# Token marks as three wide VectorE operations per set, in a decoder layer on one Trainium2 core

## The reference

```
logits = flat @ router_w.T + router_b
topk_vals, topk_idx = jax.lax.top_k(logits, TOP_K)       # 2 of 8 experts for each token
topk_w = jax.nn.softmax(topk_vals, axis=-1)
for e in range(n_exp):
    cw = jnp.sum(jnp.where(topk_idx == e, topk_w, 0.0), axis=-1)
    y = jax.nn.gelu(flat @ w1[e].T + b1[e], approximate=False)
    y = y @ w2[e].T + b2[e]
    out = out + y * cw[:, None]
x = _layernorm(x + _layernorm(out + hidden_states, ln_w, ln_b))
```

## Time and profile before

| | |
|---|---|
| median of 3 runs | 536.84 us (535.76 to 541.52) |
| the profiled execution | 537.01 us, its span 535.2 us |
| busy in the span | PE 496.5 us, PEld 446.6, DVE 367.2, ACT 261.7, POOL 268.9 |
| mean granted TensorE clock | 0.981 |

### The profile page before, as it was taken

One profiled execution on the slowest core, in us unless ns is written; L12 is line 12 of the kernel. 1 busy time (PEld: TensorE's weight loads), 2 busy tenths in 40 slices (PEclk: granted clock), 3 DMA queues, 4 the chain that ended last, 5 costly groups with the idle time before them and its releaser, 6 DMA issues.

```text
span 535.2 us, 10956 instructions
## 1 busy us (share of the span) xinstructions
PE 496.5 (93%) x3286; PEld 446.6 (83%) x3286; DVE 367.2 (69%) x1088; ACT 261.7 (49%) x861; POOL 268.9 (50%) x409
## 2 busy tenths in 40 slices
PE   5888999989999899998699999999999999999981
PEld 4667888878888788998598999999999999999970
DVE  4778867857676876448976656766676666676674
ACT  3455577765767567653233444343444334444420
POOL 4553232232332432246357657775667666676564
PEclk9899999999999999999989999999999999999997
DMA  8019930645465826445265566665566666666320
GB/s 231 12 30 352 292 107 12 234 140 168 167 198 175 276 54 252 145 167 177 90 208 198 178 208 213 223 210 204 190 199 218 226 211 225 210 202 219 138 51 1
...
## 3 DMA queue, kind: packets, MB, share of 16 engines
...
q10 hardware_dynamic: 1632, 0.27, 0.3%
...
## 4 chain that ended last, share of the span: by engine, by line
PE 34%; POOL 19%; DVE 18%; issue 17%; DMA 5%; ACT 3%; POOLq 1%; ACTq 0%; SPq 0%; DVEq 0%
PE psum_b L1569 6%; PE psum_v L1702 5%; PE psum_a L1668 5%; POOL out L809 4%; POOL routing L805 4%; POOL work L801 3%; POOL work L796 3%; POOL front_then_w_ring L752 3%; DMA weighed_outputs<-work 2%; PE psum_m L1720 2%; DVE routing L1435 2%; PE psum_b L1818 2%; PE psum_m L1569 2%; DVE work L1451 1%; PE psum_c L1689 1%
## 5 line engine op out<-in xcount | busy, mean ns | idle before, releaser
L1024 ACT ACTIVATE front_then_w_ring<-psum_b,front_then_w_ring 128x128 f32<-128x128 f32 x160 | 45.6, 368 | 72.6 <-PE psum_b L1818 72.6
L1024 ACT ACTIVATE front_then_w_ring<-psum_a,front_then_w_ring 128x128 f32<-128x128 f32 x152 | 43.2, 368 | 72.6 <-PE psum_a L1818 72.6
L1818 PEld LDWEIGHTS psum_b<-front_then_w_ring 128*128 128x128 f32 x640 | 74.5, 192 | 0.9
L1818 PE MATMUL psum_b<-front_then_w_ring 128*128 128x128 f32 x640 | 75.1, 275 | 0.0
L1818 PEld LDWEIGHTS psum_a<-front_then_w_ring 128*128 128x128 f32 x608 | 73.2, 198 | 0.9
L1818 PE MATMUL psum_a<-front_then_w_ring 128*128 128x128 f32 x608 | 73.6, 281 | 0.0
L1841 PE MATMUL psum_v<-expert_w,front_then_w_ring 128*128 x320 | 72.6, 380 | 0.2 <-issue 0.2
L912 ACT ACTIVATE work<-psum_a,score_max 128x77 f32<-128x77 f32 x256 | 62.2, 335 | 17.6 <-DVE score_max L1193 17.4
L1841 PE MATMUL psum_c<-expert_w,front_then_w_ring 128*128 x304 | 68.9, 380 | 0.1
L1841 PEld LDWEIGHTS psum_v<-expert_w,front_then_w_ring 128*128 128x128 f32 x320 | 59.5, 191 | 7.5 <-issue 0.4
L1841 PEld LDWEIGHTS psum_c<-expert_w,front_then_w_ring 128*128 128x128 f32 x304 | 56.4, 190 | 7.2 <-issue 0.4
...
## 6 DMA issues: line engine op xcount, KB each, us to landing
...
```

What stands on the lines that cost most here:

```text
L1024: last = act.activation(hidT[t % 2][:, c, :], src[:, n, q * P:(q + 1) * P], ACT.Gelu, bias=bias[:, c:c + 1])
L1818: last = pe.matmul(dst[:, n, q * P:(q + 1) * P], w1[:, k, c * P:(c + 1) * P], xtT[t % 2][:, k, :], start=(k == 0), stop=(k == KD - 1))
```

## The change

All pairs of a set are marked by three `tensor_tensor` operations over 128 x 128 x pairs elements in place of two `tensor_scalar` operations per pair: `mark_positions` and `mark_columns` compare a table of column numbers with the parts, `mark_tokens` multiplies by the token numbers in place. All operands have 2 bytes: `cols`, `token1` and `part_n` become float16, and `cols` repeats each number nine times, which makes one POOL iota of 1152 elements out of one of 128. The pair is now the innermost index of both mark arrays, so that a pair's matrix has a step of 14 or 18 elements (28 or 36 bytes) from column to column where PE reads it.

The order changes too. On PE `ranks(LAST)` moves behind `turn_rows(3)` and `down(1)`, set 1's `mark_pairs` moves behind `up(5)`, and `turn_last_tokens` behind `up(38)`. On DVE `sum_row(0)` moves ahead of `rest_map`, `sum_row(1)` ahead of `indices(3)`, and the marks of set 1 stand in two places, one operation behind `indices(3)` and two behind `sum_row(2)`. ACT, POOL and SP keep their order.

```diff
@@ -64,7 +64,7 @@
 RANKS_AT = 384
 LOGITS_AT = 320
 SET_PAIRS = tuple(TOPK * n for _, n in SETS)
-MARK_GROUPS = tuple(tuple((c * n + a, c * n + b) for c in range(TOPK) for a, b in ((0, (n + 1) // 2), ((n + 1) // 2, n))) for _, n in SETS)
+MARK_STEPS = 3
 EPS = 1e-5
 EPS_FFN = 1e-12
 MASKED = -1e30
@@ -300,8 +300,8 @@
 
         rev = tmp(E)
         slot_base = tmp(E)
-        cols = tmp(P, dt=F16)
-        token1 = tmp(TILES)
+        cols = tmp(P, TILES - FIRST, dt=F16)
+        token1 = tmp(TILES, dt=F16)
         token_off = tmp(TILES)
         tau = tmp(XS_TILES, E - 1)
         tau_row = tau[:, :, 0]
@@ -325,12 +325,12 @@
         higher = tmp(TILES, E)
         slot_i = tmp(TOPK, TILES, dt=I32)
         part_i = tmp(TOPK * TOPK, TILES, dt=I32)
-        part_n = tmp(TOPK * TOPK, TILES)
+        part_n = tmp(TOPK * TOPK, TILES, dt=F16)
         ext = tmp(TILES, E, EXT)
         mark_words = SET_PAIRS[0] * P // 2
 
         def marks(ap):
-            return ap.bitcast(F16).rearrange("p (i m) -> p i m", m=P)
+            return ap.bitcast(F16).rearrange("p (m i) -> p m i", m=P)
 
         late_words = SET_PAIRS[1] * P // 2
         at_pos = [marks(LATE[:, 0:mark_words]), marks(SECOND[:, 0:late_words])]
@@ -672,7 +672,7 @@
                       allow_small_or_imprecise_dtypes=True).then_inc(route_consts, 1)
             pool.iota(slot_base, pattern=[[PER_E * P, E]], base=1, channel_multiplier=0,
                       allow_small_or_imprecise_dtypes=True).then_inc(route_consts, 1)
-            pool.iota(cols, pattern=[[1, P]], base=0, channel_multiplier=0,
+            pool.iota(cols, pattern=[[1, P], [0, TILES - FIRST]], base=0, channel_multiplier=0,
                       allow_small_or_imprecise_dtypes=True).then_inc(route_consts, 1)
             pool.iota(token1, pattern=[[P, TILES]], base=1, channel_multiplier=1,
                       allow_small_or_imprecise_dtypes=True).then_inc(route_consts, 1)
@@ -1241,8 +1241,12 @@
                 if H == RANKS_STEP + 8:
                     dve.wait_ge(pos_mm, 1)
                     dve.tensor_copy(first_token_of, table_psum(0)).then_inc(table_ready, 1)
-                if RANKS_STEP + 3 <= H < RANKS_STEP + 3 + len(MARK_GROUPS[0]):
-                    mark_rows(0, *MARK_GROUPS[0][H - RANKS_STEP - 3])
+                if H == RANKS_STEP + 3:
+                    mark_positions(0)
+                if H == RANKS_STEP + 4:
+                    mark_columns(0)
+                if H == RANKS_STEP + 5:
+                    mark_tokens(0)
             steps = [0]
 
             def then(ins):
@@ -1370,17 +1374,34 @@
                 dve.wait_ge(map_ready, MAPS)
                 map_of(tbend, spare, XS_TILES, e_base)
 
-            def mark_rows(n, first_pair, end):
+            def pairs_of(ap, n):
+                return ap.rearrange("p m (c t) -> p m c t", c=TOPK)
+
+            def over_pairs(n):
+                return [P, P, TOPK, SETS[n][1]]
+
+            def numbers(n):
+                nt = SETS[n][1]
+                return cols[:, :, 0:nt].rearrange("p m (c t) -> p m c t", c=1).to_broadcast(over_pairs(n))
+
+            def parts(n, half):
                 t0, nt = SETS[n]
+                part = part_n[:, half * TOPK:(half + 1) * TOPK, t0:t0 + nt]
+                return part.rearrange("p (m c) t -> p m c t", m=1).to_broadcast(over_pairs(n))
+
+            def mark_positions(n):
                 if n == 0:
                     dve.wait_ge(qT_ready, NP)
-                for i in range(first_pair, end):
-                    c, j = divmod(i, nt)
-                    t = t0 + j
-                    dve.tensor_scalar(at_pos[n][:, i], cols, part_n[:, c, t:t + 1], None, ALU.is_equal)
-                    last = dve.tensor_scalar(at_col[n][:, i], cols, part_n[:, TOPK + c, t:t + 1], token1[:, t:t + 1],
-                                             ALU.is_equal, ALU.mult)
-                last.then_inc(pos_ready, 1)
+                dve.tensor_tensor(pairs_of(at_pos[n], n), numbers(n), parts(n, 0), ALU.is_equal).then_inc(pos_ready, 1)
+
+            def mark_columns(n):
+                dve.tensor_tensor(pairs_of(at_col[n], n), numbers(n), parts(n, 1), ALU.is_equal).then_inc(pos_ready, 1)
+
+            def mark_tokens(n):
+                t0, nt = SETS[n]
+                tokens = token1[:, t0:t0 + nt].rearrange("p (m c t) -> p m c t", m=1, c=1).to_broadcast(over_pairs(n))
+                dve.wait_ge(pos_ready, n * MARK_STEPS + 2)
+                dve.tensor_tensor(pairs_of(at_col[n], n), pairs_of(at_col[n], n), tokens, ALU.mult).then_inc(pos_ready, 1)
 
             for p in range(3):
                 input_moments(p)
@@ -1474,19 +1495,17 @@
             first_hot(LAST)
             second_choice(LAST)
             dve.memset(token_of[:, P:COLS], 0.0)
+            sum_row(0)
             rest_map()
             ranked(LAST)
             place(LAST)
             dve.wait_ge(ln_in, 2 * 16)
             weigh_output(1)
             add_input(1)
-            sum_row(0)
-            mark_rows(LAST, *MARK_GROUPS[LAST][0])
             row(inner_norm(0))
+            sum_row(1)
             indices(3)
-            sum_row(1)
-            mark_rows(LAST, *MARK_GROUPS[LAST][1])
-            mark_rows(LAST, *MARK_GROUPS[LAST][2])
+            mark_positions(LAST)
             def last_tokens():
                 dve.wait_ge(load_ready, SLOT_TILES)
                 for n in range(2):
@@ -1529,7 +1548,8 @@
                 add_input(t)
                 sum_row(t)
                 if t == 2:
-                    mark_rows(LAST, *MARK_GROUPS[LAST][3])
+                    mark_columns(LAST)
+                    mark_tokens(LAST)
                     later_map()
                 if t == FIRST - 4:
                     dve.wait_ge(pos_mm, LAST + 1)
@@ -1773,10 +1793,9 @@
                 last.then_inc(rank_mm, 1)
 
             def mark_pairs(n):
-                for g, (first_pair, end) in enumerate(MARK_GROUPS[n]):
-                    pe.wait_ge(pos_ready, n * len(MARK_GROUPS[0]) + g + 1)
-                    for i in range(first_pair, end):
-                        last = pe.matmul(table_psum(n), at_pos[n][:, i], at_col[n][:, i], start=(i == 0), stop=(i == SET_PAIRS[n] - 1))
+                pe.wait_ge(pos_ready, (n + 1) * MARK_STEPS)
+                for i in range(SET_PAIRS[n]):
+                    last = pe.matmul(table_psum(n), at_pos[n][:, :, i], at_col[n][:, :, i], start=(i == 0), stop=(i == SET_PAIRS[n] - 1))
                 last.then_inc(pos_mm, 1)
 
             normalised(0)
@@ -1862,23 +1881,21 @@
             up(2, 0)
             route_logits(TILES - 1)
             up(2, 1)
-            pe.wait_ge(lg_ready, TILES)
-            ranks(LAST)
             turn_rows(3)
             down(1)
+            ranks(LAST)
             for t in range(3, SLOT_TILES):
-                if t == FIRST - 2:
-                    pe.wait_ge(placed, 3 * LAST + 1)
-                    mark_pairs(LAST)
                 up(t, 0)
                 up(t, 1)
+                if t == FIRST - 2:
+                    mark_pairs(LAST)
+                if t == LAST_TILE:
+                    turn_last_tokens()
                 if t + 1 < SLOT_TILES:
                     turn_rows(t + 1)
                 if t - 1 == FIRST:
                     pe.wait_ge(map_ready, 2 * MAPS)
                 down(t - 1)
-                if t == LAST_TILE - 1:
-                    turn_last_tokens()
             down(SLOT_TILES - 1)
```

## The result

| | before | after |
|---|---|---|
| median of 4 runs | 537.10 us (535.76 to 541.52) | 548.96 us (548.12 to 550.00) |
| profiled execution | 537.01 us, span 535.2 | 548.74 us, span 547.0 |
| PE / DVE / POOL busy | 496.5 / 367.2 / 268.9 | 505.0 / 360.3 / 277.5 |
| mean granted clock | 0.981 | 0.970 |

The ratio is 1.0207 (95%: 1.0169 to 1.0244): slower by 11.9 us, where no change was forecast. The marks did get cheaper, and VectorE is busy 7 us less. The time went elsewhere.

The account below looks back on a forecast made before the run. The chain from `weigh_output(3)` through tile 7's gather was taken to bound the stretch, TensorE from there on. 537.01 + 0.0 (A) - 1.1 (B) + 2.4 (C) - 1.2 (D) = 537.1; forecast 537.0 us, range 531.5 to 541.5.

Parts of the forecast that it names:

- The iota, costed at nothing: Among GpSimd's early constants: the longer iota is free since GpSimd idles half the span; 1.1 us without that cover.
- A, the strided product: Set 0, attention loop: wide marks gain 0.3 us, strided product costs 0.3; 0.0 in all (-0.5 to +3.6).
- signs of being wrong: Tile 7's gather issued before 274 us, marks over 2 us, or mark products over 0.1 us apart.
- B, tile 7: Set 1: fewer marks between `sum_row(1)` and `weigh_output(3)` bring `turn_rows(7)` earlier; gain of 1.1 us, capped by a gather.
- C, the clock: TensorE waits 5.8 us ahead of `turn_rows(7)` and its clock falls uncovered behind it: +2.4 us (0 to 3.6).
- D, the end: Kernel end: `up(38)` covers the 1.76 us wait of `turn_last_tokens`, last weighing earlier: -1.2 us (-2 to 0).
- The slower one: Wide marks at one element a step also hold GpSimd's gathers: 542.3 us, 544.7 with a clock fall; chance 0.08.

Follow-up runs that it names:

- e2: The changed kernel with its iota of 1152 elements moved into an idle GpSimd stretch of the attention loop; 543.12 us, ratio 1.0092.
- e7: e2 with set 1's rank product and the sums of rows 0 and 1 back in their old places; 541.80 us, ratio 1.0073.
- e9: The kernel before with wide marks and strided product in set 1 only, later mark product and last-token transpose, longer iota at 102 us; 534.56 us, ratio 0.9953.
- e1: The kernel before with its iota writing 1152 elements as nine runs of 128; 538.45 us, ratio 1.0042.
- e5: The kernel before plus the change's own iota (each number nine times in a row) into a tile nothing reads; 544.76 us, ratio 1.0107.
- g2: e7 with set 0's strided mark product issued twice; 545.65 us, ratio 1.0124.
- e6: The kernel before with its narrow marks stored with the change's step between elements; 547.97 us, ratio 1.0179.
- g1: e9 with set 0's dense mark product issued four times; 537.27 us, ratio 0.9977.
- e4: The kernel before with narrow marks in their old layout, but all the change's moves on PE and DVE; 542.98 us, ratio 1.0101.
- d1: The kernel before with only `turn_last_tokens` moved behind `up(38)`; 537.12 us, ratio 0.9965.
- e3: The changed kernel with marks stored pair by pair, a zero step in the wide operations, iota back to 128 elements; 543.65 us, ratio 1.0119.

## Why the prediction was wrong

The moves in the medians of all runs, one edit after the other: 549.0 after, 543.1 with the iota moved (e2), 541.8 with ranks and row sums back (e7), 534.6 with set 0 as before (e9). Two terms of the sum carry the miss, the iota and the strided product of set 0.

**The iota, costed at nothing: +6.0 us.** This is the first step that failed. The prediction put the longer iota under "GpSimd is idle for half of the span", and priced it without that cover at 1.1 us. Both were wrong, and for different reasons. The cover is a mean over the span; at 37 us POOL goes from the constants to the key weighing without a pause, and PE waits for it. I never looked at the row. And the price of 1.04 ns an element was VectorE's. It is near GpSimd's only for long runs: 9 runs of 128 took 1.13 us (e1), where 128 elements took 0.23, but 128 runs of 9 took 3.75 (e5). The iotas behind the dear one overlap it in the trace, and from L660 to the key weighing it is 3.5 us more in all. The rest is the clock, which falls behind the longer wait. e5 and e2 show it from both sides.

**A, the strided product: +0.8 us in the profile and about 7 in the medians, where 0.0 was forecast.** The marks were right: 1.22 us against 1.1, and c-d grows by 2.0 us, so without the product's 2.5 it gains 0.5 (0.3 forecast). Part of the 2.5 is hidden, since PE would have waited for the first gather of token rows. The product was taken at 0.3, near the lower end of 0 to 2.4, and the upper end was true. The argument for the lower end, that float32 products keep to 0.12 us, says nothing about a step: those read without one. By the Trainium skill, "SBUF — State Buffer", section "Specifications (TRN2)", an access that gets less than two hits out of a 16-byte line is slowed; with steps of 28 and 36 bytes there is one. The trace agrees: 0.23 us against 0.056. The prediction cited that rule and did not let it move the term, though products over 0.1 us apart stand among its own signs of being wrong.
What the section on A did not have at all: the clock can fall behind such a product (e2, g2), 3 us more. With it A is 4 us; the other 3 of the 7 us between e7 and e9 are not accounted for.

**B, tile 7: +1.8 us where -1.1 was forecast.** By its own steps: from `sum_row(1)` to `weigh_output(3)` 15.1 us were forecast, 15.8 came (marks of 1.55 us, not 1.35). But `sum_row(1)` was to be 0.25 us later and was 2.6 (15.26 against 12.68 behind the choice). The sentence that failed is that VectorE's wait "is filled by `sum_row(0)`". It took the gather of row 0 as landed. The ranks came as forecast (2.08 us behind the choice) and were done at 255.5, when that gather had only just landed: `sum_row(0)` then ran ahead of `rest_map`, 1.0 us. With it `load_base(1)` is issued 1.35 us later, not 0.25. The rest of the 2.6 is its gather, which took 5.7 us, not 4.4; it is 5.6 to 6.1 in all five profiles with the row sum ahead and 3.9 to 4.8 in the eight others, leaving out e6 with its slow marks. Why it takes longer was not isolated. In those five e-f is 14.3 to 15.3 us. In the eight it is 12.3 to 14.2, and the three over 13.5 (e1, g1, g2) have a granted clock of 0.66 to 0.87 over 5 us or more there, so the groups do not overlap at full clock (12.3 to 13.1). With the row sum back and wide marks in set 1, e-g is 0.9 and 1.0 us shorter than before in e7 and e9, and 0.7 and 0.3 in g1 and g2; the 1.1 of step B was about right.

**C, the clock: right in kind, absent here.** It needs a long wait at tile 7. e4 has one of 3.2 us and pays 2.6 us for it in `down(6)`, against 2.4 forecast. In the changed kernel the wait at `up(5)`, the product of 4.4 us and the slow `down(4)` used up that time first.

**D, the end: -1.0 us in the profile, -1.2 forecast** (d1). The wait at the transpose is gone, as said.

**Rivals.** The slower one named the wide marks at one element a step; with the pairs innermost they take 1.55 us for 2304 elements, 0.67 ns each, and reach 1.04 ns only with a step of zero (e3). By the Trainium skill, "VectorE: DVE Perf Modes", section "The perf-mode tier table", two elements a cycle is the most for this form, 1224 ns for 2048 elements. An estimate by that page's figure is 1.38 us for 2304. The trace agrees roughly: they took 1.55. Its other half did show, VectorE's operations holding GpSimd: beside a wide mark POOL's root takes 1.95 us in place of 0.72. What this costs the kernel was not measured.

```profile
276.67 1.55 DVE L1398 TENSOR_TENSOR second_buffers<-routing 128x2304 f16<-128x2304 f16 x1
```

```profile
276.84 1.95 POOL L805 TENSOR_TENSOR routing<-routing,minus_half 128x2 f32<-128x2 f32 x1 [0.52 <-DVE routing L1458]
```

No rival had the loss at 45 us, where 6 of the 11.9 us arise. The chance of slower was set at 0.08 with one mechanism counted; a change that makes two things cheaper on VectorE by making GpSimd write more and TensorE read with a step deserved a case for each.

Left open: some 4 of the 11.9 us, which the stretches do not give to an edit. The start, where the clock fell for longer in the profile after, and a clock that falls behind set 0's product in some runs are the candidates. Why the clock fell from 20 to 40 us in some executions and not in others, with the same code, is open too.
